# Bank words of the adjacency loaded in eights, and the last stage of a four-layer graph network rearranged

## What is computed

```python
x = layernorm(x + gcn(x))        # three graph convolutions, each with layer norm and relu
x = layernorm(x + sum_of_neighbours(x @ W.T + b))
x = layernorm(x + gin(x))        # (1 + eps) x + neighbours, two dense layers with batch norm
x = layernorm(x + rgcn(x))       # two relational layers, 8 edge types

def rgcn_layer(x, src, dst, etype, W, W_root, b, num_rels):
    h = jnp.einsum('ni,rio->rno', x, W)
    msg = h[etype, src]
    seg = dst * num_rels + etype
    sums = jax.ops.segment_sum(msg, seg, num_segments=N * num_rels)
    cnt = jax.ops.segment_sum(jnp.ones(msg.shape[0], x.dtype), seg, num_segments=N * num_rels)
    mean = sums / jnp.maximum(cnt, 1.0)[:, None]
    return mean.reshape(N, num_rels, do).sum(axis=1) + x @ W_root + b
```

## Time and profile before

| | us |
|---|---|
| median of 3 runs | 3812.71 (3811.78 to 3816.45) |
| the profiled execution | 3823.57 |
| its span, first to last instruction | 3821.7 |
| mean granted clock of PE | 0.743 of full speed |
| PE, DVE, POOL, ACT busy | 2532.7, 2517.1, 1959.8, 485.3 |
| adjacency stage, L445 | from 99.5 to 481 |
| last stage, from inv to the last instruction | 3760.8 to 3821.7 |

### The profile page before, as it was taken

The page is one execution under the profiler, slowest core; times in us unless marked ns, Lnnn a source line. Parts: engine busy times, 40 slices in busy tenths (PEclk is TensorE's granted clock), DMA queues, the critical chain, the costliest instruction groups (busy, mean ns, idle before and its releaser), DMA issues.

```text
span 3821.7 us, 59833 instructions
## 1 busy us (share of the span) xinstructions
PE 2532.7 (66%) x21427; PEld 1819.2 (48%) x21427; DVE 2517.1 (66%) x6311; ACT 485.3 (13%) x906; POOL 1959.8 (51%) x2108
## 2 busy tenths in 40 slices
PE   3766689989746565666555558965555655656556
PEld 1222265574435444444444446754444444444446
DVE  5999954464267666666666666666666666666667
ACT  2444441151110000000000003510000000000000
POOL 1887800000256666666666662146666666666661
PEclk9999989989865666566666668966666666666667
DMA  1000000000111111111111111111111111111111
GB/s 51 1 1 1 1 6 1 1 2 1 39 52 44 45 44 45 44 45 44 45 45 45 45 45 49 75 60 44 45 44 45 44 45 44 45 45 45 44 45 32
DMA packets 76098, 137.92 MB, mean 36 GB/s; under 512 B 29902, under 2 KB 44640, under 8 KB 75810
## 3 DMA queue, kind: packets, MB, share of 16 engines
q0 software_dynamic: 53120, 108.90, 10.9%
q1 hardware_dynamic: 18934, 24.46, 1.8%
q10 hardware_dynamic: 3756, 0.73, 0.2%
HBM read 116.35 MB, written 17.62 MB: 35 GB/s over the span
## 4 chain that ended last, share of the span: by engine, by line
PE 45%; DVE 28%; issue 11%; another core or an unknown queue 8%; POOL 3%; DMA 2%; ACT 2%; DVEq 1%; ACTq 1%; SPq 0%; POOLq 0%
PE banks L565 26%; DVE adj L1429 15%; DVE hi_hot L1131 6%; PE banks L497 6%; PE banks L490 3%; DVE lo_hot L1139 3%; PE banks L609 2%; POOL adj L711 2%; PE banks L621 2%; DMA adj<-table,adj 2%; PE banks L654 1%; DVEq L1427 1%; PE banks L472 1%; POOL lo_hot L685 1%
## 5 line engine op out<-in xcount | busy, mean ns | idle before, releaser
L565 PE MATMUL banks<-adj 128*128 128x129 f16 x13280 | 1486.3, 291 | 1026.5 <-DVE adj L1429 739.7
L711 POOL DMA_INDIRECT adj<-table,adj x1660 | 1573.3, 948 | 946.8 <-issue 402.1
L565 PEld LDWEIGHTS banks<-adj 128*128 128x128 f16 x13280 | 1199.5, 132 | 1317.9 <-issue 1161.6
L1429 DVE TENSOR_TENSOR adj<-adj,banks 128x516 f32 x1660 | 1143.0, 689 | 844.5 <-PE banks L565 480.7
L1413 DVE TENSOR_SCALAR adj<-adj 128x512 f16<-128x512 f16 x1660 | 697.1, 420 | 0.0
L685 POOL TENSOR_SCALAR lo_hot<-minus_iota,zT 128x128 f16<-128x128 f16 x392 | 332.4, 865 | 140.4 <-PE banks L445 77.1
L445 PE MATMUL banks<-hi_hot,lo_hot 128*128 128x400 f16 x977 | 267.0, 365 | 128.0 <-DVE hi_hot L1131 73.5
L1131 DVE TENSOR_SCALAR hi_hot<-iota,zT 128x400 f16<-128x400 f16 x977 | 266.0, 338 | 21.5 <-PE banks L445 21.4
L692 POOL MEMSET adj<- 128x1548 f16 x1 | 1.4, 1388 | 470.4 <-PE banks L497 470.4
L445 PEld LDWEIGHTS banks<-hi_hot,lo_hot 128*128 128x128 f16 x977 | 97.4, 100 | 297.9 <-issue 240.4
L497 PE MATMUL banks<-adj,split 128*128 128x512 f16 (+1 forms) x1190 | 235.7, 356 | 0.0
(11 more groups left out here) (219 smaller groups left out, 1625.6 us busy)
## 6 DMA issues: line engine op xcount, KB each, us to landing
adj<-table,adj POOLq DMA_INDIRECT x1660
table<-adj SPq DMA_DIRECT2D x25, 512.0 KB, 2.6
table<-split SPq DMA_DIRECT2D x6, 256.0 KB, 2.3
out_dram<-xres SPq DMA_DIRECT2D x6, 256.0 KB
adj<-in_L_gnn_W_dram SPq DMA_DIRECT2D x1, 1024.0 KB, 7.4
adj<-in_L_gnn_W_dram SPq DMA_DIRECT2D x2, 512.0 KB, 9.0
adj<-scr_index SPq DMA_DIRECT2D x1, 830.0 KB
scr_index<-adj SPq DMA_DIRECT2D x1, 512.0 KB
```

The costliest lines, as they stand in the source:

```text
L565: m = e.matmul(ps[:, g * CH // 2:g * CH // 2 + b - a], hot[:, s, g * P:g * P + P], gath[:, s, a:b], start=(q == 0), stop=(q == 1), skip_gr ...
L711: e.indirect_dma_start(gath[:, s, 0:2 * D], None, table, bass.IndirectOffsetOnAxis(ap=index[:, which, j:j + 1].bitcast(U32), axis=0)).then ...
L1429: e.tensor_tensor(a, a, ps[:, :].rearrange("p (g d) -> p g d", g=G)[:, :, 0:D + 1], ALU.add).then_inc(accumulated, 1)
```

## The change

It has two parts.

1. PE's bank words are loaded eight at a time (WORDS = 8), at every 64th step: 16 loads for 4. SP's, ACT's and DVE's loads keep 32.
2. The last stage. DVE's `inv` is announced to ACT and POOL (`inv_set`). For each window ACT scales slot 0 (even windows) or slots 0 and 1 (odd windows), POOL scales slot 2, and DVE multiplies slot 3 by its inv and adds POOL's slot 2 in one operation, and in even windows slot 1 and ACT's slot 0 in the same way. PE adds root_out by `ident` and then two slots (even window) or three (odd) for each window into one of 25 places in banks 0 to 6, so no place is used twice. DVE takes the statistics from PSUM. The parameters are made for blocks 0 to 15 as soon as block 15's statistics are there, and for blocks 16 to 24 at the end; ACT normalizes the first 16 blocks and 16, 19 and 22, DVE the six others, all from PSUM.

```diff
--- before.py
+++ after.py
@@ -18,6 +18,7 @@
 WR, WR_LOG2 = 64, 6
 REGS = 32
 POOL_SHARE = (2, 5)
+WORDS = 8
 FIELDS = 8
 AHEAD = 4
 FX = 1024.0
@@ -283,7 +284,8 @@
         hid_sum, hid_relu, hid_high, hid_low, tab_sum, root_sum, tab_high, tab_low, root_read, root_ready = (
             sem(n) for n in ("hid_sum", "hid_relu", "hid_high", "hid_low", "tab_sum", "root_sum", "tab_high", "tab_low",
                              "root_read", "root_ready"))
-        placed, place_read = sem("placed"), sem("place_read")
+        inv_set, scaled_act, scaled_pool, slots_added, placed, stats_read = (
+            sem(n) for n in ("inv_set", "scaled_act", "scaled_pool", "slots_added", "placed", "stats_read"))
 
         PICKS = [(0, a0, min(CH, JA - a0)) for a0 in range(0, JA, CH)]
         NADJ = len(PICKS)
@@ -324,6 +326,23 @@
         SQUARES.append(("R2", bank[7], [sqr]))
 
         NB_ODD, NB_EVEN = NB // 2, NB - NB // 2
+        FRONT = 4
+
+        def final_by_act(b):
+            return b < 4 * FRONT or (b - 4 * FRONT) % (7 - FRONT) == 0
+
+        def slots_of(w):
+
+
+            mine = ((0,), (1, 3), (1, 3)) if w % 2 == 0 else ((0, 1), (3,), (0, 1, 3))
+            return mine + (w + 1 + (w + 1) // 2, 2 * (w + 1) - (w + 1) // 2)
+
+        def final_place(b):
+
+            k, n, first = (b, FRONT, 0) if b < 4 * FRONT else (b - 4 * FRONT, 7 - FRONT, FRONT)
+            at = k // n * P
+            return (b - n if k >= n else None), bank[first + k % n][:, at:at + D]
+
         LATE = 4 * EARLY
         LATE_ODD = NB_ODD - LATE // 2
         NORM_ACT_LAST = 2 * LATE_ODD + NB_ODD + LATE_ODD + NB_ODD
@@ -389,8 +408,8 @@
             n_dve, n_act = 0, 0
             for i, quad in enumerate(quads):
                 q0, q1 = quad[0], quad[-1] + 1
-                n_dve += sum(b % 2 == 0 for b in quad)
-                n_act += sum(b % 2 for b in quad)
+                n_act += sum(final_by_act(b) for b in quad)
+                n_dve += sum(not final_by_act(b) for b in quad)
                 e.wait_ge(norm_dve, NORM_DVE_LAST + n_dve)
                 e.wait_ge(norm_act, NORM_ACT_LAST + n_act)
                 if i < NQ - 1:
@@ -427,12 +446,12 @@
                             if q == TILE:
                                 m.then_inc(picked, 1)
 
-            words = [e.alloc_register(f"banks_of{i}") for i in range(REGS)]
+            words = [e.alloc_register(f"banks_of{i}") for i in range(WORDS)]
             e.wait_ge(words_set, 1)
             for j in range(JA):
                 g, w = j // LG, j // FIELDS
-                if j % (FIELDS * REGS) == 0:
-                    n = min(REGS, NWORD - w)
+                if j % (FIELDS * WORDS) == 0:
+                    n = min(WORDS, NWORD - w)
                     e.load(words[0:n], word_row[:, w:w + n])
                 if j % 4 == 0:
                     e.wait_ge(gate, j // 4 + 1)
@@ -440,7 +459,7 @@
                     e.wait_ge(low_pool if by_pool(g) else low_dve, low_at[g])
                 if j % 2 == 0:
                     e.wait_ge(high, min(j + 2, JA))
-                word = e.snap(words[w % REGS], min_val=0, max_val=NWIN ** FIELDS - 1)
+                word = e.snap(words[w % WORDS], min_val=0, max_val=NWIN ** FIELDS - 1)
                 c = word // NWIN ** (j % FIELDS) % NWIN
                 e.matmul(banks[:, bass.ds(c, 1), 0:NC].rearrange("p o n -> p (o n)"), lo_hot[:, g % NLO, j % LG, :],
                          hi_hot[:, j % NHI, :], start=False, stop=True, skip_group_check=True).then_inc(crossed, 1)
@@ -645,14 +664,20 @@
             e.wait_ge(tab_low, 2 * NB)
             scatter(1)
             e.wait_ge(place_set, WPB * P // WR)
+            e.wait_ge(root_ready, 1)
+            e.wait_ge(accumulated, 2 * JR)
             for nb in range(NB):
-                g0, c = nb * GB, nb % 4
-                e.wait_ge(row_scaled, NB + nb + 1)
-                if nb >= 4:
-                    e.wait_ge(place_read, nb - 3)
-                for q in range(GB):
-                    m = e.matmul(bank[2 * c][:, 0:D], place[:, q, :], sums_g[:, g0 + q, 0:D], start=(q == 0),
-                                 stop=(q == GB - 1))
+                before, to = final_place(nb)
+                if before is not None:
+                    e.wait_ge(stats_read, before + 1)
+                e.matmul(to, ident[:, :], root_out[:, nb, :], start=True, stop=False, skip_group_check=True)
+                for w in range(nb * WPB, (nb + 1) * WPB):
+                    _, _, slots, act_at, dve_at = slots_of(w)
+                    e.wait_ge(scaled_act, act_at)
+                    e.wait_ge(slots_added, dve_at)
+                    for g in slots:
+                        m = e.matmul(to, place[:, w % WPB * G, :], sums[:, w, g, 0:D], start=False,
+                                     stop=(w % WPB == WPB - 1 and g == 3), skip_group_check=True)
                 m.then_inc(placed, 1)
 
         @block.gpsimd
@@ -724,6 +749,10 @@
             for s in range(2):
                 e.wait_ge(table2_out[s], 16 * ((NB - s + 1) // 2))
             gather(1, table2)
+            e.wait_ge(inv_set, 2)
+            for w in range(NW4):
+                e.tensor_scalar(sums[:, w, 2, 0:D], sums[:, w, 2, 0:D], inv[:, w * G + 2:w * G + 3], None,
+                                ALU.mult).then_inc(scaled_pool, 1)
 
         @block.scalar
         def _(e):
@@ -958,10 +987,24 @@
                     turn_rows(nb + 2)
                 table_rows(nb)
 
-            sqrt(NB)
+            e.wait_ge(inv_set, 2)
+            for w in range(NW4):
+                for g in slots_of(w)[0]:
+                    e.activation(sums[:, w, g, 0:D], sums[:, w, g, 0:D], ACT.Identity,
+                                 scale=inv[:, w * G + g:w * G + g + 1]).then_inc(scaled_act, 1)
+
+            def final_rows(b0, b1):
+                for b in range(b0, b1):
+                    if final_by_act(b):
+                        e.activation(xres[:, b, :], final_place(b)[1], ACT.Identity,
+                                     bias=nmr[:, b:b + 1], scale=rstd[:, b:b + 1]).then_inc(norm_act, 1)
+
+            sqrt(4 * FRONT)
             e.wait_ge(normed, 11)
-            for quad in quads:
-                normalize(xres, znode, quad)
+            final_rows(0, 4 * FRONT)
+            sqrt(NB - 4 * FRONT)
+            e.wait_ge(normed, 12)
+            final_rows(4 * FRONT, NB)
 
         @block.vector
         def _(e):
@@ -1438,8 +1481,8 @@
                 e.wait_ge(own_dve, own.up())
                 e.reciprocal(inv[:, :], inv[:, :]).then_inc(own_dve, 1)
                 e.wait_ge(own_dve, own.up())
-                e.tensor_scalar(inv[:, :], inv[:, :], factor, None, ALU.mult).then_inc(own_dve, 1)
-                e.wait_ge(own_dve, own.up())
+                e.tensor_scalar(inv[:, :], inv[:, :], factor, None, ALU.mult).then_inc(inv_set, 1)
+                e.wait_ge(inv_set, which + 1)
 
             SUMMED = {}
             total = 0
@@ -1587,23 +1630,37 @@
             e.tensor_tensor(root_out, root_out, xres[:, :, :], ALU.add).then_inc(root_ready, 1)
             e.wait_ge(sums_zero, 1 + NB)
             relation_sums(1, scales[:, 1, 3:4])
-            e.wait_ge(root_ready, 1)
-            scale_rows(0)
-            scale_rows(1)
+
+            def add_slots(w):
+                for g in slots_of(w)[1]:
+                    if g == 1:
+                        e.wait_ge(scaled_act, slots_of(w)[3])
+                    else:
+                        e.wait_ge(scaled_pool, w + 1)
+                    e.scalar_tensor_tensor(out=sums[:, w, g, 0:D], in0=sums[:, w, g, 0:D],
+                                           scalar=inv[:, w * G + g:w * G + g + 1], in1=sums[:, w, g - 1, 0:D],
+                                           op0=ALU.mult, op1=ALU.add).then_inc(slots_added, 1)
+
+            def final_stats(b):
+                e.wait_ge(placed, b + 1)
+                e.bn_stats(stats[:, b, :], final_place(b)[1]).then_inc(stats_read, 1)
+                e.wait_ge(stats_read, b + 1)
+                e.bn_aggr(mv[:, b, :], stats[:, b, :]).then_inc(own_dve, 1)
+                own.up()
+
+            for w in range(2 * WPB):
+                add_slots(w)
             for nb in range(NB):
-                if nb + 2 < NB:
-                    scale_rows(nb + 2)
-                e.wait_ge(placed, nb + 1)
-                e.tensor_tensor(root_out[:, nb, :], root_out[:, nb, :], bank[2 * (nb % 4)][:, 0:D],
-                                ALU.add).then_inc(place_read, 1)
-                if nb:
-                    e.wait_ge(place_read, nb)
-                    stats_of(znode, [nb - 1], {nb - 1: own.n})
-            e.wait_ge(place_read, NB)
-            stats_of(znode, [NB - 1], {NB - 1: own.n})
-            norm_params()
-            for quad in quads:
-                normalize(xres, znode, quad)
+                for w in range((nb + 2) * WPB, min((nb + 3) * WPB, NW4)):
+                    add_slots(w)
+                final_stats(nb)
```

(7 more changed lines are left out.)

## The result

The kernel after takes 3786.73 us (median, 3785.86 to 3787.78), the kernel before 3814.24 us on the same chip (3811.78 to 3816.45): 27.5 us less, a ratio of 0.9928 (95% interval 0.9911 to 0.9945). The forecast was 3788.9. That it is only 2.2 us off is in part luck: it had started from 3812.7 for the kernel before, and of the gain it missed 3.7 us (23.8 forecast). The profiled execution took 3787.01 us, with a span of 3785.1 and a mean granted clock of 0.740.

The account below looks back on a forecast made before the run. No engine was busy over two thirds of the span; DVE bound the adjacency stage except where PE stopped. Adjacency 13.5, placing 5.6, tail 4.0, output 0.7: 23.8 us off 3812.7 gave 3788.9; own range 3780 to 3798, with rivals 3779 to 3803.

Parts of the forecast that it names:

- Adjacency, 13.5 us: Adjacency stage: shorter word loads, covered by DVE's run-on, gain 13.5 us (4.5 to 16.5).
- DVE's idle time, 2 us for the loads and 1 for POOL: Adjacency stage: of 16.5 us of idle time, 2 stay at loads and 1 goes to POOL being late.
- A block of 1.34 us on PE: Last stage: six matmuls per block of two windows instead of eight, 0.224 us each, so 1.34 us.
- POOL 0.68 a scaling: Last stage: each POOL scaling takes 0.68 us (0.60 to 0.93), two per block, 1.36 us.
- The adds of DVE: Last stage: three scale-and-adds per block at 0.21 us each; with statistics, DVE needs 1.05 us a block.
- The stop at block 15: Last stage: DVE waits for ACT's square root behind all 75 scalings; PE then rests 4.4 us after block 17.
- ACT: 0.385 us: Last stage: ACT's scalings come 0.385 us apart, priced from its normalizations; 28.9 us for all 75.
- The rival: Last stage, chance 0.13: ACT's scalings 0.30 us apart, no stop at block 15, placing ends 5.6 us earlier; 3783.3 us.
- DVE and POOL shutting each other out: Last stage, chance 0.15: POOL scalings and DVE adds never overlap; PE ends 11.1 us later than forecast; 3800.0 us.
- Loads not covered: Adjacency stage, chance 0.07: DVE stands for each whole load, 26.5 us replacing 16.5; 3812.4 us.
- POOL starving: Last stage, chance 0.05: POOL scalings take 1.83 us each, so PE ends 45.0 us later than before; 3839.5 us.
- Tail, 4.0: After the last placement: less statistics work and fewer normalizations left gain 4.0 us (3.3 to 4.4).

Follow-up runs that it names:

- e1: Kernel before with only the word loads changed to eight words each; 3770.38 us, ratio 0.9965.
- e7b: Kernel after, but each load, still at every 64th step, fetches 16 words and only eight are used; one execution, 3781.35 us against 3785.62.
- e6: Kernel after with 16 words a load on PE; ratio 0.9960 against before.
- e3: Kernel after with a bias column of zeros given to ACT's 75 scalings; 3763.05 us, ratio 0.9949 against before.
- e2: Kernel after with the loads of before, 32 words each, so only the last stage is changed; 3768.99 us, ratio 0.9962 against before.
- e8: Kernel after with ten filler matmuls into an unused bank before and just behind the first placement; 3786.01 us, ratio 0.9923 against before.
- e4: Kernel after with DVE's adds held back until POOL has made all its 50 scalings; one execution, 3780.91 us.
- e9: e8 with ACT also scaling slot 2 in every fourth window, so POOL has 38 scalings and ACT 87; 3755.03 us, ratio 0.9921 against before.

## Why the prediction was right or wrong, step by step

- **Adjacency, 13.5 us: right** (13.6; 12.4 in e1). Its terms: load of eight words 1.89 us, measured 1.93. DVE's idle time, 2 us for the loads and 1 for POOL: measured 4.4 without the start, of which 1.4 came from POOL. e7b and e6 confirm the mechanism: 2.0 us of stop for a load of 3.8.
- **A block of 1.34 us on PE: exact.** POOL 0.68 a scaling: 0.664. The adds of DVE were mis-sized, 0.21 forecast and 0.25 measured (0.27 beside POOL), since an addition's row had been used for a multiply-add with a scalar column. DVE needs 1.22 us a block and not 1.05, still under PE's 1.34, so it cost nothing.
- **The stop at block 15: absent, and this is the step that failed.** The text had said that its absence would make it wrong. The mistake is the term "ACT: 0.385 us": it took the row of the normalizations, which have a bias column. Without one they came 0.293 us apart, 22.0 us for 75 and not 28.9, and ACT was free 4.23 us before DVE asked. The rival had this number (0.30, 22.5 us), and no row of before could decide. With the bias column (e3) the stop, PE's rest and the end of placing came within 1.2 us of the forecast.
- **The rival's 36.5 us to the end of placing: 38.5.** The terms that the text gives for it make 0.95 + 1.6 + 25 x 1.34 = 36.05; the other 0.45 has no term. PE started 1.4 us after T0 and not 0.95 (0.5), the low clock cost 3.0 us and not 1.6 (1.4), and 0.78 went to the parameter chain. The 1.6 was one profile's figure: before, PE had been at 1.00 by 3766, under 4 us after its start; here that took more than 5 us, from 3739.75 to about 3745. It isn't a difference of the two kernels that is shown, since the last stage of before lost 2.9 us in e1, and that of after 1.9 in e2 and 3.2 in e6. So placing ended 3.6 us before the forecast and not 5.6. e8 shows that a full clock alone wouldn't have helped: POOL takes 2.2 of the 3.0 us, and PE's longer rest behind block 17 1.2.
- **DVE and POOL shutting each other out: fallen** (e4). **Loads not covered: fallen**, DVE idles 0.2 us and not 1.89 a load. **POOL starving: fallen.**
- **Tail, 4.0: 3.7.** DVE's six normalizations from PSUM took 2.01 us and not 1.6: the price had been that of rows from SBUF. After the last normalization 1.1 us were gained (0.7).
- **Sum.** 13.6 + 9.2 + 3.7 + 1.1 = 27.6 against 23.8. The absence of the stop is worth more than the whole difference; the other misses took part of it back. So for the last stage the time came near by luck: its main wait wasn't there.

## What to carry to other kernels

A wait forecast on an in-order engine is as good as the pace of what is queued before it: price each operation with a row of its own form, down to the operands, and where no row has it, say at which price the wait goes. When engines run near each other's pace, as PE, POOL and DVE do here at 1.34, 1.33 and 1.22 us a block, relieving one gives nothing until the waits behind it are relieved as well. And before a difference of 1 us in a stage is put down to an edit, look at the same stage in the other runs in which it is unchanged. A register load in front of a matmul costs only what exceeds the work its producer can run ahead with, so cut it to that length; cutting further gave no gain that the runs settle.

## What the runs showed of the hardware

- An ACTIVATE of 128x128 f32 with a scale column takes 386 ns (0.293 us from one to the next); with a bias column too, 480 ns (0.385), even when the column is zero.
- PE's register load from SBUF takes 0.234 us a word, with under 0.07 us fixed: 0.767 us for 3 words and 7.545 for 32. The first load of a kernel took longer (3.41 us for 8 words).
- Beside DVE's multiply-adds of two 128x128 f32 operands in SBUF, a POOL scaling takes 0.664 us on the average and up to 0.942, and 0.58 without them; with the PE clock at 1.00 throughout, the average was 0.713 (e8). The adds are slowed by 0.01 us. ACT's scalings beside POOL changed nothing (e4); PE's part wasn't tried.
- After its 1.90 us of rest in e9, PE's granted clock fell to 0.50 again, as it did after 3.90 us in e3; after 1.95 us in e8, and after the 0.78 us in the kernel after (the ten records behind it took 1.35 us), it did not.
- The same instructions in the same order spend different times at the low clock: it cost 1.9 us of the last stage in e2 and 3.2 in e6.
